# Issuing an attention pair's first scores in alternation with the next pair's second scores on TensorE

## The reference

```python
# second attention: 16 heads of 8, rotary positions, no mask
q, k, v = split_heads(x), split_heads(c_k @ w_uk + b_uk), split_heads(c_v @ w_uv + b_uv)
q, k = _apply_rope(q, cos, sin), _apply_rope(k, cos, sin)
attn = softmax(einsum('bhid,bhjd->bhij', q, k) / sqrt(8), axis=-1)
out = einsum('bhij,bhjd->bhid', attn, v).transpose(0, 2, 1, 3).reshape(B, T, D)
x = _layernorm(x + out @ w_o + b_o)
...
# second router: the two best of eight experts for each row
gates = x @ router_w + router_b
topv, topi = jax.lax.top_k(gates, 2)
```

## Time and profile before

| | |
|---|---|
| median of three runs | 1437.58 us (1434.99 to 1444.62) |
| the profiled execution | 1433.81 us, span 1431.9 us |
| mean granted TensorE clock over the span | 0.92 |
| second attention, from the maxima added in iteration 2 to those added in iteration 15 | 840.05 to 1194.06 us: 13 iterations in 354.01 us, 27.23 us each |

### The profile page before, as it was taken

The page is one execution under the profiler, slowest core; times in us unless marked ns, Lnnn a source line. Parts: engine busy times, 40 slices in busy tenths (PEclk is TensorE's granted clock), DMA queues, the critical chain, the costliest instruction groups (busy, mean ns, idle before and its releaser), DMA issues. The chain is left out here.

```text
span 1431.9 us, 33756 instructions
## 1 busy us (share of the span) xinstructions
PE 1295.6 (90%) x10829; PEld 1053.9 (74%) x10829; DVE 957.0 (67%) x2849; ACT 863.9 (60%) x2233; POOL 617.5 (43%) x965
## 2 busy tenths in 40 slices
PE   6999999999999999799997898898889888978877
PEld 5888888888888888799996565555555554756765
DVE  6787877777787887667775667767766753543323
ACT  4777777776777766356643555555554544846643
POOL 3244444444444444435534345444543422435553
PEclk9999999999999999899998679878877975989998
DMA  7020202020312210132131222022050002022215
GB/s 259 20 89 26 86 26 86 30 88 28 97 46 73 83 54 17 55 113 65 57 129 52 76 76 78 21 83 75 22 196 8 13 13 82 18 82 80 78 53 184
DMA packets 56451, 100.88 MB, mean 70 GB/s; under 512 B 11056, under 2 KB 46256, under 8 KB 53616
## 3 DMA queue, kind: packets, MB, share of 16 engines
q1 hardware_dynamic: 46704, 80.06, 17.5%
q0 software_dynamic: 9088, 18.89, 3.8%
q10 hardware_dynamic: 576, 0.86, 0.2%
HBM read 78.81 MB, written 62.06 MB: 98 GB/s over the span
## 5 line engine op out<-in xcount | busy, mean ns | idle before, releaser
L622 ACT ACTIVATE a_prob<-psum,a_nmx 128x128 f32<-128x128 f32 (+1 forms) x512 | 208.3, 425 | 72.8 <-DVE a_nmx L985 72.8
L855 POOL TENSOR_TENSOR a_prob<-a_prob,a_rl 128x128 f32<-128x128 f32 (+1 forms) x256 | 124.3, 507 | 241.7 <-DVE a_rl L989 241.0
L2664 DVE TENSOR_REDUCE f_nmx<-psum 128x4 f32<-128x1024 f32 x120 | 147.0, 1225 | 56.1 <-PE psum L214 52.3
L2418 ACT ACTIVATE a_prob<-psum 128x1024 f32<-128x1024 f32 x128 | 130.9, 1023 | 36.9 <-PE psum L2150 34.0
L629 ACT ACTIVATE a_probt<-psum 128x768 f32<-128x768 f32 x128 | 104.8, 819 | 79.5 <-PE psum L1432 79.5
L902 POOL DMA_INDIRECT yt<-a_yrow,a_dest x78 | 79.4, 1018 | 106.9 <-ACT a_yrow L671 89.4
L622 ACT ACTIVATION_READ_ACCUMULATOR a_prob<-psum,a_nmx 128x1 f32 x512 | 107.9, 211 | 0.0
L1432 PE MATMUL psum<-ident,a_prob 128*128 128x128 f32 x768 | 105.3, 273 | 1.1 <-DVE a_prob L995 0.7
L1789 POOL DMA_INDIRECT yt<-m_yrow,m_dest x78 | 76.1, 975 | 69.7 <-DVE m_yrow L1936 45.7
L974 DVE TENSOR_TENSOR a_qkt<-psum,a_bqk 128x512 f32<-128x512 f32 x128 | 88.2, 689 | 26.3 <-PE psum L109 23.7
L2160 PE MATMUL psum<-a_prob,a_v 128*32 128x256 f32 x1024 | 94.5, 502 | 1.4 <-DVEq L2726 1.3
(11 more groups left out here) (411 smaller groups left out, 3838.6 us busy)
## 6 DMA issues: line engine op xcount, KB each, us to landing
xs<-in_fill SPq DMA_DIRECT2D x144, 264.0 KB, 4.2
a_xrow<-xs SPq DMA_DIRECT2D x39, 132.0 KB
m_xrow<-xs SPq DMA_DIRECT2D x39, 132.0 KB
f_yin<-yt SPq DMA_DIRECT2D x18, 256.0 KB, 2.9
w<-in_w SPq DMA_DIRECT2D x16, 256.0 KB, 3.4
f_yin<-yt SPq DMA_DIRECT2D x7, 512.0 KB, 8.0
f_w<-in_wr SPq DMA_DIRECT2D x2, 1284.0 KB
xs<-in_fill_idle SPq DMA_DIRECT2D x2, 1056.0 KB, 6.3
```

The lines of the kernel that those rows point to most:

```text
L622: last = nc.scalar.activation(prob[:, hp % 4, h, at], S[:, 2 * (hp % 2) + h, at], ACT.Exp, bias=nmx[:, hp % 4, q, h:h + 1], accum_out=lsum ...
L855: last = nc.gpsimd.tensor_tensor(prob[:, hp % 4, 0, at], prob[:, hp % 4, 0, at], rl[:, hp % 4, 0, q:q + 1].to_broadcast(prob[:, hp % 4, 0, ...
L2418: nc.scalar.activation(prob[:, k % 2, 2 * (t % 2):2 * (t % 2) + 2, :], ST[:, 2 * (t % 2):2 * (t % 2) + 2, :], ACT.Exp, scale=SCALE).then_i ...
L2664: nc.vector.reduce_max(f.nmx[:, :, 2 * i:2 * i + 2].rearrange("p q h -> p h q"), R.rearrange("p h (q k) -> p h q k", q=QB), AX.X, negate=T ...
```

## The change

In TensorE's program the first scores of pair i and the second scores of pair i+1 become one block in alternation, two matmuls of each in turn, for i = 1 to 6; the block waits for both conditions before it begins. Pair 0, pair 7 and the second scores of pairs 0 and 1 stay by themselves. `outputs(0)` now stands behind the block of pair 2, `outputs(1)` behind that of pair 4, `outputs(2)` behind that of pair 5. `tail_rows` moves behind the block of pair 3, and `tail_project` comes ahead of pair 2. In VectorE's program `route_rows` goes from ahead of `maximum(4)` to behind it, and `ranked` from ahead of `maximum(7)` to behind `split_maxima`. The waits of `outputs(1)` and of the last `outputs` stay as they are.

```diff
+            def part_of_pair(i, q, p):
+                for c in range(2):
+                    last = first_scores(2 * i + c, q, p, R[:, c, :])
+                return last
+            def part_of_scores(t, k, p):
+                for h in (2 * t, 2 * t + 1):
...
+                    def pair_and_scores(i, t):
+                        if second:
+                            may_pair(i)
+                        pe.wait_ge(exp_done, n * NPR + t - 1)
+                        if not second:
+                            scores(t)
+                            return
+                        part_of_pair(i, 0, 1 - p)
+                        part_of_scores(t, 0, p)
+                        part_of_pair(i, 1, 1 - p).then_inc(pair_ps, 1)
+                        part_of_scores(t, 1, p).then_inc(st_ps, 1)
...
-                    pe.wait_ge(exp_done, n * NPR + 4)
-                    scores(5, p)
-                    first(4)
+                    pair_and_scores(4, 5)
                     if routed:
                         pe.wait_ge(lt_done, n - 1)
                     outputs(1, p, n)
-                    pe.wait_ge(exp_done, n * NPR + 5)
-                    scores(6, p)
-                    first(5)
+                    pair_and_scores(5, 6)
...
# VectorE
+                    maximum(4)
                     if routed:
                         route_rows(n - 1, PV)
-                    maximum(4)
...
-                    if routed:
-                        ranked(n - 1, PV)
                     maximum(7)
                     if second:
                         dve.wait_ge(pair_done, n * NPR + NPR)
                         split_maxima()
+                    if routed:
+                        ranked(n - 1, PV)
```

More of the change, by code:

```diff
@@ L2136, in two_stacks @@
                 stack(k + 1, banks[:, 1, :]).then_inc(both_ps, 1)
[L2138 to L2152, removed]
+            def part_of_pair(i, q, p):
[4 more added lines that the diff above has]
+                for h in (2 * t, 2 * t + 1):
+                    rows = slice(LOW * (h % HG), LOW * (h % HG + 1))
+                    last = nc.tensor.matmul(ST[:, 2 * (t % 2) + h % 2, k * T:(k + 1) * T], stk[p][rows, h // HG, 1, k * P:(k + 1) * P],
+                                            stk[p][rows, h // HG, 0, :], start=True, stop=True)
+                return last
             def outputs(k, p, n):
@@ L2228, in batches, with may_pair, pair, scores @@
                     tail = follows(n)
-                    def first(i):
-                        if second:
[L2232 to L2238, removed]
+                    def may_pair(i):
+                        if i == 0:
+                            pe.wait_ge(both_act, n * 2 + 2)
+                        elif i == NPR // 2 and turned:
+                            pe.wait_ge(both_act, n * 2 + 3)
+                        else:
+                            pe.wait_ge(pair_done, n * NPR + i)
+                    def pair(i):
+                        if second:
+                            may_pair(i)
+                            part_of_pair(i, 0, 1 - p)
+                            part_of_pair(i, 1, 1 - p).then_inc(pair_ps, 1)
+                    def scores(t):
+                        part_of_scores(t, 0, p)
+                        part_of_scores(t, 1, p).then_inc(st_ps, 1)
+                    def pair_and_scores(i, t):
+                        if second:
+                            may_pair(i)
+                        pe.wait_ge(exp_done, n * NPR + t - 1)
+                        if not second:
+                            scores(t)
+                            return
+                        part_of_pair(i, 0, 1 - p)
+                        part_of_scores(t, 0, p)
+                        part_of_pair(i, 1, 1 - p).then_inc(pair_ps, 1)
+                        part_of_scores(t, 1, p).then_inc(st_ps, 1)
                     if second:
@@ L2260, in batches @@
                         pe.wait_ge(both_act, 1)
-                    scores(0, p)
+                    scores(0)
                     if tail:
@@ L2266, in batches @@
                         pe.wait_ge(osb_done, n * NGR + 1)
-                    first(0)
+                    pair(0)
                     if routed:
@@ L2271, in batches @@
                         pe.wait_ge(o_done, n + 1)
-                    scores(1, p)
-                    first(1)
+                    scores(1)
                     if second:
@@ L2279, in batches @@
                         tail_columns(n + 1, MISC)
-                    pe.wait_ge(exp_done, n * NPR + 1)
-                    scores(2, p)
-                    first(2)
+                    pair_and_scores(1, 2)
                     if tail:
                         tail_project(columns_of(n - 1), n + 1)
[L2285 to L2290, removed]
+                    pair_and_scores(2, 3)
                     if routed:
@@ L2294, in batches @@
                     outputs(0, p, n)
-                    pe.wait_ge(exp_done, n * NPR + 3)
-                    scores(4, p)
+                    pair_and_scores(3, 4)
+                    if tail:
+                        pe.wait_ge(rt_done, n + 1)
+                        tail_rows(n + 1)
                     if routed:
@@ L2321, in batches @@
                     outputs(2, p, n)
-                    scores(7, p)
-                    first(6)
+                    pair_and_scores(6, 7)
                     if fresh:
@@ L2326, in batches @@
                         latents(columns_of(n + 3), n + 4)
-                    first(7)
+                    pair(7)
                     if routed:
```

## The result

The changed kernel takes 1465.01 us (median of four runs, 1462.91 to 1473.07) where the kernel before takes 1440.07 (four runs, 1434.99 to 1444.62): a ratio of 1.0184 with an interval of 1.0130 to 1.0239. The profiled execution took 1466.04 us with a span of 1464.3, 32.4 us more than the span before. The forecast was 1456.

A forecast was written before the change was run, and what follows sets the result against it. Bound by a chain through the two banks R: matmuls write, VectorE reads, then the next user writes. Profiled 1433.8 + 12.7 (steps) + 8 (clock) = 1454.5, forecast 1456 as median; 1444 to 1466 has 0.5, 1434 to 1478 holds 8 in 10.

The forecast's parts named there:

- M_2 to M_4: From start of `maxima(2)` to `maxima(4)`: stacks start sooner after pair 3; -1.3 us with half clock, -0.3 at full.
- `tail_project`: Ahead of pair 2 on TensorE: delays the chain by 0.1 us at full clock, up to 0.3 us otherwise.
- M_4 to M_5: From start of `maxima(4)` to `maxima(5)`: `outputs(1)` waits for late `route_rows`, pair 5 queues behind; +1.1 to +1.9 us.
- M_6 to M_7: From start of `maxima(6)` to `maxima(7)`: VectorE no longer waits for `ranks` behind pair 7; -0.7 us.
- M_7 to the next add: From start of `maxima(7)` to the next add: last `outputs` waits for late `ranked`, stacks follow; +2.0 us.
- The rest: Other stretches of the iteration, add to `maxima(0)` and `maxima(5)` to `maxima(6)` among them: stays as it is.
- three signs named for a wrong forecast: Last `outputs` within 0.5 us of `maxima(7)`; `maxima(5)` 1.83 us after `maxima(4)`; iteration no longer at same half-clock time.
- The clock: TensorE's clock over the thirteen iterations: thinner stretches add 2 us at half clock in each, +8 us; granted clock below 0.82.
- The clock takes more: Rival: second clock fall at the iteration's end, 6.9 us more at half, 27 us over 13 iterations, 1474; chance 0.2.
- The draw: Rival: half-clock stretch before `maxima(4)` gains more, -0.8 more per iteration, clock adds nothing, 1436.5; chance 0.2.
- Faster, the two waits do not bite: Rival: waits before `outputs(1)` and last `outputs` hidden, only gains before `maxima(4)` and `maxima(7)` left, -29, 1405; chance 0.1.
- Alternation by itself: Turns of pair and score matmuls on TensorE: no gain taken, though halving a pair's 0.50 us would give about 20 us.

The follow-up runs named there:

- first comparison: Runs on one chip where the kernel before takes 1394.92 us; both VectorE steps put back early in the changed kernel there: 1361.56 us, 0.9779.
- third: Runs on another chip where the kernel before takes 1441.94 us; both VectorE steps put back early in the changed kernel there: 1427.08 us, 0.9885.
- the runs with one step moved: Changed kernel with one VectorE step put back early: only `route_rows`, 1389.42 us, 0.9966; only `ranked`, 1390.07 us, 0.9968.
- the old order: Kernel before with only VectorE's two moves (`route_rows` and `ranked` late), TensorE's program unchanged: 1431.22 us, 1.0266.
- the rows early: Changed kernel with `route_rows` back ahead of `maximum(4)`, `ranked` still behind the split: 1389.42 us, 0.9966.
- the order alone: Changed kernel with `route_rows` and `ranked` both back at their old places: 1361.56 us, 0.9779; on another chip 1427.08 us, 0.9885.
- the pair of runs without turns: Changed kernel, both VectorE steps back early, each block four matmuls of the pair then four of the scores: 1420.50 us, 0.9868; again 1424.24 us, 0.9882.
- second and third comparison: Two sets of runs, each on one chip, with the kernel before at 1437.25 us and 1441.94 us.
- `tail_project`'s run above: Changed kernel with both VectorE steps back early and `tail_project` behind the block of pair 2: 1429.28 us, 0.9933.

## Why the prediction was nearly right, and where not

The sign and the cause were right: 1456 forecast, 1465 measured, inside the range and at the edge of the forecast's own spread. Steps by the means of the table:

1. **M_2 to M_4** (forecast -1.3): M_3 to M_4 went from 6.92 to 5.12, M_2 to M_3 by -0.06, together -1.86. The stacks do start when M_3 ends, and at half clock M_3 to M_4 is 5.73, forecast 5.7. The mean is better than forecast since the stretch is now at the full clock in six iterations instead of one; there the change is worth 0.1 us (4.80 to 4.69). But its term for **`tail_project`** was mis-sized: put at 0.1 to 0.3 us, it measured +0.79 in M_1 to M_2. The price was taken as TensorE's own time. What costs is that `tail_project` waits for ScalarE's copy of a_ot, and pair 2 is queued behind it. ScalarE after, ahead of that copy:

```profile
1019.59 1.00 ACT L2425 ACTIVATE a_prob<-psum 128x1024 f32<-128x1024 f32 x1
1020.50 0.40 ACT L2459 ACTIVATE f_qk_h<-f_rq 128x256 fp32r<-128x256 f32 x1
1020.80 0.36 ACT L2434 ACTIVATE a_ot<-psum 128x256 f32<-128x256 f32 x1
```

   The transposes it needs were issued at 1018.75; the copy stands behind an exponential and a rotated operand, and TensorE has been idle for 1.25 us when it ends. With it, step 1 is -1.1. Not all of the 0.79 is the new place: with both VectorE steps early M_1 to M_2 is 2.15 (first comparison) and 2.33 (third), and TensorE waits 7.0 us for the copy in thirteen iterations, not 11.3. Why the late steps delay it further is not taken apart.
2. **M_4 to M_5** (forecast +1.1, bound +1.9): +1.83. The mechanism is shown by the runs with one step moved; the term was mis-sized, since I let `outputs(1)` run at the full clock, as it did in the iteration I read the earlier trace rows. The one iteration where this stretch is at 1.00 has 2.91 us, forecast 2.97; in the twelve others, 0.50 to 0.66, it is 4.06 or 4.07. The wait has its forecast place, 1.36 us behind M_4 to 1032.22.
3. **M_6 to M_7** (-0.7): -0.71.
4. **M_7 to the next add** (+2.0): +2.11; the last `outputs` 2.21 us behind M_7, forecast 2.3. At the full clock the stretch is 4.7 to 4.9 us (forecast 5.0, "M_7 + 5.0"), against 3.0 to 3.2 before, so the wait by itself is +1.8; the rest is mostly the four iterations of 6.4 to 6.5 us where the clock fell.
5. **The rest** (0): +0.07, -0.07 and +0.14 in the other three.

These make +2.30 an iteration where +1.1 to +2.1 stood, and the other parts of the program, where I had -2.6 for iterations 0 and 1 alone, came to +2.3 (-3.9, +1.9 and +4.3). None of the three signs named for a wrong forecast showed: the last `outputs` starts 2.21 us behind M_7, M_5 is 3.97 us behind M_4, and an iteration with the same time at half clock is longer (30.05 us at 0.77, from 1014.54, against 28.04 at 0.76). The 4.3 us behind the thirteen iterations is not taken apart. The two profiled executions differ by 32.2 us, the medians by 24.9, and the forecast rise was 20.7: part of what the steps show beyond the forecast lies in which executions were profiled.

**The clock** (+8 us, "less than 0.82"): not borne out as a step of its own. The granted clock is 0.82 before and after in the thirteen iterations, and the time at half clock rose by 1.1 us each, where I had 2; at 0.3 us apiece 1.1 x 0.3 x 13 = 4.3. What I had wrong is the picture: the clock is not a sum on top of the steps but sits inside them. It left M_3 to M_4 and came to M_4 to M_5, which makes step 1 better and step 2 worse than forecast. Over thirteen iterations step 2 was some 9 us too low and `tail_project` some 8, M_3 to M_4 and M_2 to M_3 some 7 too high, and the 8 us of the clock were counted apart; that these cancel in part is luck. The Trainium skill (TensorE: Matmul & The Clock Gate, A second HAM failure mode: psum-queue depth-cycling) says that small idles between groups of matmuls make the clock swing and cost throughput. By that rule, the trace agrees for the waits taken alone (0.950 to 0.939 and 0.935 over whole runs, 0.917 to 0.905 in the old order), but not for the change as a whole, whose order gives the same amount back.

**The rivals.** "The clock takes more" as the main cause falls with 0.82 in both; but the second fall at the end of the iteration that it names is there in four iterations after the change (two before), and in nine of thirteen with the rows early. The draw falls with the 95% interval, though its reasoning, that step 1 is worth more, was right by 0.6 us for M_2 to M_4. "Faster, the two waits do not bite" falls by the waits themselves, 13 of 13 iterations; but the order without them is indeed faster: -33.4 us on one chip, -14.9 on another. That this lies around the rival's -29 is chance: it counted on step 3, which the order alone does not have (M_6 to M_7 is 2.62).

**Alternation by itself.** I gave the turns no gain, and the pair of runs without turns shows none. After the change eight matmuls hold TensorE for 0.44 us (1022.07 to 1022.51), where four of one pair took 0.43. The Trainium skill (TensorEngine Tiling (Array Packing), Theoretical Speedup) states up to 4x for such a contraction. The two pairs of bands give 2x here over one pair, and the program before had that already at pair 6. What the order gains is its places: `outputs(0)` under M_2 and no second scores between pair 3 and the stacks, which counts at half clock (7.55 to 5.73 us) and hardly at full (4.80 to 4.69).

**Open.** On the chips of the second and third comparison, M_0 to M_1 is 2.2 to 2.4 us on the mean in all five kernels with the new order and early VectorE steps, where it is 1.8 in the first comparison and in the changed kernel. In the rows of `tail_project`'s run above, the last recorded matmuls of pair 1 start at 1006.30 and take 0.28 us, yet M_1 starts at 1007.48, 0.9 us after their end. It is up to 0.6 us x 13 = 8 us of the difference between 0.978 and 0.989 for one and the same kernel. No run here tells its cause.

## What to carry over

A step that an in-order engine waits for has two prices: its own time, and the wait for its operands. Before moving it ahead of the critical block, look up when the engine that supplies it is through, here a reduction of 1.23 us on VectorE or an exponential on ScalarE. Moving consumers' order and producers' places in one change hides a gain behind a loss: here the order alone is 1.1 to 2.2% faster than the kernel before, and the two late steps made it 1.8% slower. Where every cover is nearly full, a step taken out of the way of one pair stands in the way of the next, by its own time or by what is queued behind it, as the runs with `tail_project`, `ranks` and `outputs(1)` moved showed.

## What the runs showed that was not expected

- The same program differs by 3% between chips (1395, 1437 and 1442 us), and the gain of one edit by a factor of two (0.978 and 0.989). The intervals within one comparison are 0.2 to 0.6% each way and say nothing of that.
- Which order the program issues matmuls of different bands in does not matter: 1424.24 and 1427.08 us, and starts 0.01 us apart in both.
- The clock follows how the waits lie, at the same work: 0.76 to 0.91 over the thirteen iterations on one chip, with 2463 matmul records in each. What a step costs depends on which clock it meets: the same `outputs(1)` behind the same wait made M_4 to M_5 2.91 us or 4.06.
